# Value projections without a staging transpose, an early context sum, and a reordered output loop in an 8-core attention and gating kernel

## The chip, the cores and the metric

The kernel runs on all 8 cores of one Trainium2 chip. Each core computes one of the eight batch entries of 4096 tokens by 1024 features, with no exchange between cores. The metric is the device time in microseconds of the slowest core.

## The reference

Per batch entry (x is 4096 by 1024; 16 heads of 64; every token attends to every token, with an ALiBi bias that grows with the key's position):

```python
xn = _layernorm(x)
kqv = xn @ W_kqv.T                       # k, q, v
score = q @ k.T / sqrt(1024) + slope[h] * (n - s)
s = softmax(score) @ v
gf = global_net(xn.mean(tokens))         # 1024 -> 512 -> 256 -> 1
out = xn
for _ in range(3):
    tf = coupling_net(out)               # 1024 -> 1024 -> 512 -> 256 -> 1
    coupling = 0.1 + ar * (0.7 * gf + 0.3 * tf - 0.5) * 2.0
    out = out + coupling * twist(out)
x = x + s * silu(out)
```

## The kernel before

All stages use hand-placed buffers and hand-written semaphores. Each engine has one instruction stream, and each stream keeps the order in which the Python code emits it.

**Normalisation.** Tokens are loaded in slabs of 512, normalised, transposed by TensorE in 128x128 blocks, and cast by VectorE (L312) into XB, the bf16 transposed activations (features on partitions, 4096 tokens along the row).

**Attention.** Heads are worked in 8 pairs. `kqv_units(p, b)` is a generator that makes the projections of pair p, one unit for each `yield`. A "kq" unit is 8 accumulating matmuls of 512 tokens (L399) and one VectorE cast (L406). A "vt" unit is 8 accumulating matmuls (L416) that give V transposed for 512 tokens, a VectorE copy to VSTG (L423) and, emitted one unit later by `flush_vt`, four f32 transposes (L372) and two casts (L377) into the V buffer. `attn_units(p, b)` is the attention of pair p: for each block of 128 keys and each head two score matmuls (L474) and two exponentials on ScalarE (L482), and, one step later, two value matmuls a head (L456, L458). After each pass over the keys VectorE copies the sums out (L502). The four half banks of PA and PC form one ring (`ring_next`), which scores, projections and V transposes share. A unit or a score tile can start only when its half bank has been read.

Heads with steep slopes look at the last key blocks only. The first key block of a pair, N0_PAIR, is 30, 29, 27, 23, 15, 0, 0, 0 for pairs 0 to 7, of 32 blocks. So the pairs have 1, 1, 2, 3, 5, 8, 8, 8 vt units, 36 in all. The driving loop emits pair 0's units first, all at once, and then the units of pair p+1 between the steps of pair p, at 48/na units a step with na = 4 (34 - N0_PAIR[p]); a loop behind the steps emits what is left. V units come last in each pair's list.

**Context sum.** `gctx_chunk(p)` puts two VectorE sums over XB's rows (L321, 4096 elements each) behind each of the pairs 0 to 3; the eighth is followed by a small scaling. The result is used only after the attention.

**Feed-forward.** STATE, the f32 transposed activations, is rebuilt from x, and three cycles of 8 chunks of 512 tokens go through the coupling net (L721, L754, L775) and update STATE (L828, L837).

**Output.** 16 chunks of 256 tokens. ACT's queue loads the attention sums (SINB, 1024 KB, two buffers, L870). For each of 8 feature tiles: POOL multiplies STATE by SINB into FTMP (L881, two buffers), TensorE spreads the reciprocal of the softmax sums over the partitions (L893), VectorE multiplies the two into SG (L903, one buffer). Then for each half k of 128 tokens: SP loads the rows of x (XT, 512 KB, L914) as soon as the addition that last used this buffer is over, TensorE makes 8 transposes of SG (L921), VectorE adds (L929), SP stores (L933).

Of the kernel before, what the change touches and what calls it, by code (L numbers as in the profile page):

```python
# [6 lines left out]
F32 = mybir.dt.float32  # L7
BF16 = mybir.dt.bfloat16
AF = mybir.ActivationFunctionType
AOP = mybir.AluOpType  # L10

S, D, H, HD = 4096, 1024, 16, 64
NT = S // 128
NF = D // 128
# [3 lines left out]
NTC = S // TC  # L18
# [27 lines left out]
def build_program(debug=False):  # L46
# [76 lines left out]
    def at(name, shape, dtype, off_kib):  # L123
        t = nc.alloc_sbuf_tensor_at(name, shape, dtype, offset=A0 + int(off_kib * KIB))
        return t.ap()
# [7 lines left out]
    VB = [at(f"VB{i}", [128, 32 * 130], BF16, 144 + 8.25 * i) for i in range(2)]  # L133
    PB_ = [at(f"PBUF{i}", [128, 512], BF16, 160.5 + 1 * i) for i in range(12)]
    SRW = [at(f"SRW{i}", [128, 1024], F32, 172.5 + 4 * i) for i in range(2)]
    VSTG = [at(f"VSTG{i}", [128, 512], F32, 180.5 + 2 * i) for i in range(2)]
    vsj = [0]
    STATE = at("STATE", [128, NF * S], F32, 0)
    XT2s = [at(f"XT2s{i}", [128, 2 * D], F32, 128 + 8 * i) for i in range(2)]
    XNF2 = [at(f"XNF2{i}", [128, D], F32, 144 + 4 * i) for i in range(4)]  # L140
# [9 lines left out]
    TCF = 256  # L150
# [70 lines left out]
    with nc.Block() as block:  # L221
# [38 lines left out]
        for sl in range(NSLAB):  # L260
# [37 lines left out]
            for b in range(4):  # L298
                i = 4 * sl + b
                for g in range(2):  # L300
# [11 lines left out]
                    inst = VE.tensor_copy(out=dst, in_=src)  # L312
                    vXBe.inc(inst)
                    lnslot_tok[slot] = vXBe.n
        def gctx_chunk(pi):
            if pi >= 4:
                return
            if pi == 0:
                VE.wait_ge(vXBe.h, vXBe.n)
            for ft in range(2 * pi, 2 * pi + 2):  # L320
                VE.reduce_sum(gct[:, ft:ft + 1], XB[:, ft * S:(ft + 1) * S], axis=mybir.AxisListType.X)  # L321
            if pi == 3:
                VE.drain()
                inst = VE.tensor_scalar(out=gctb[:], in0=gct[:], scalar1=1.0 / S,
                                        scalar2=None, op0=AOP.mult)
                vGctx.inc(inst)

        TE.wait_ge(sW.h, W0_TOTAL)
        TE.wait_ge(sWG.h, WG_TOTAL)
# [9 lines left out]
        def ring_next():  # L339
            r = ring_pos[0]  # L340
            ring_pos[0] = (r + 1) % 4
            if ring_tok[r] is not None:
                sem, val = ring_tok[r]
                TE.wait_ge(sem.h, val)
            return r
# [8 lines left out]
        def kqv_units(p, b, prologue=False, prev2=None):  # L354
            first = [True]

            def gate_ve():
                if first[0]:
                    if prev2 is not None:
                        VE.wait_ge(tAV.h, pair_tok[prev2])  # L360
                    first[0] = False

            n0p = N0_PAIR[p]
            pvt = []

            def flush_vt():
                while pvt:
                    j, cp_tok, sc = pvt.pop(0)
                    r2 = ring_next()
                    TE.wait_ge(vKV.h, cp_tok)  # L370
                    for k in range(4):
                        inst = TE.transpose(RING[r2][:, k * 128:(k + 1) * 128],  # L372
                                            VSTG[j][:, k * 128:(k + 1) * 128], identf[:])
                    tKQ.inc(inst)
                    VE.wait_ge(tKQ.h, tKQ.n)
                    for hh in range(2):
                        inst = VE.tensor_copy(  # L377
                            out=v4[b][:, 4 * sc:4 * sc + 4, hh, 0:64],
                            in_=RING[r2].rearrange("p (k d) -> p k d", d=128)[:, :, hh * 64:hh * 64 + 64])
                        vKV.inc(inst)  # L380
                    ring_tok[r2] = (vKV, vKV.n)

            units = []
            for fpi, fp in enumerate([8 + p, p]):
                tc0 = (n0p * 128) // 512 if fpi == 1 else 0
                for tc in range(tc0, NTC):
                    units.append(("kq", fpi, fp, tc, 4 * (tc + 1)))
            for sc in range(n0p // 4, NTC):
                units.append(("vt", 0, 0, sc, 4 * (sc + 1)))
            if prologue:  # L390
                units.sort(key=lambda u: (u[4], u[0]))
            for kind, fpi, fp, tc, need in units:
                r = ring_next()
                if prologue:
                    TE.wait_ge(vXBe.h, min(2 * need, 64))
                if kind == "kq":
                    dst = QT[b] if fpi == 0 else KT[b]
                    for ft in range(NF):
                        inst = TE.matmul(RING[r],  # L399
                                         WK[:, ft * 3 * D + fp * 128: ft * 3 * D + (fp + 1) * 128],  # L400
                                         XB[:, ft * S + tc * 512: ft * S + (tc + 1) * 512],
                                         start=(ft == 0), stop=(ft == NF - 1))
                    tKQ.inc(inst)
                    gate_ve()
                    VE.wait_ge(tKQ.h, tKQ.n)
                    inst = VE.tensor_copy(out=dst[:, tc * 512:(tc + 1) * 512], in_=RING[r])  # L406
                    vKV.inc(inst)
                    ring_tok[r] = (vKV, vKV.n)
                    flush_vt()
                else:  # L410
                    sc = tc
                    base = 2 * D + p * 128
                    j = vsj[0] % 2
                    vsj[0] += 1
                    for ft in range(NF):
                        inst = TE.matmul(RING[r],  # L416
                                         WK[:, ft * 3 * D + base: ft * 3 * D + base + 128],
                                         XB[:, ft * S + sc * 512: ft * S + (sc + 1) * 512],
                                         start=(ft == 0), stop=(ft == NF - 1))
                    tKQ.inc(inst)  # L420
                    gate_ve()
                    VE.wait_ge(tKQ.h, tKQ.n)
                    inst = VE.tensor_copy(out=VSTG[j][:], in_=RING[r])  # L423
                    vKV.inc(inst)
                    ring_tok[r] = (vKV, vKV.n)
                    flush_vt()
                    pvt.append((j, vKV.n, sc))
                yield
            flush_vt()

        SC2 = 512
        NSCP = 4
# [87 lines left out]
        for p in range(8):  # L520
# [19 lines left out]
                    gen_k = None  # L540
            if p < 7:
                kqv_tok[p + 1] = vKV.n
            gctx_chunk(p)

        GP.wait_ge(tAV.h, tAV.n)
        GP.wait_ge(vSR.h, vSR.n)
# [317 lines left out]
        for tch in range(NTCF):  # L864
# [3 lines left out]
            if tch == 0:  # L868
# [3 lines left out]
                         .rearrange("(ft p) s -> p ft s", p=128)  # L872
                         ).then_inc(sSIND[sb6].h, 16)
            sSIND[sb6].n += 16
            for ft in range(NF):
                b2_ = sg_idx % 2
                GP.wait_ge(sSIND[sb6].h, sSIND[sb6].n)
# [13 lines left out]
                if sg_idx >= 4:  # L891
                    TE.wait_ge(vTT2.h, sg_idx - 4 + 1)
                inst = TE.matmul(HALF[slot][:, 0:TCF], sel[:, ft * 128:(ft + 1) * 128],  # L893
                                 RD[0:16, tch * TCF:(tch + 1) * TCF], start=True, stop=True)
                tRDB.inc(inst)
                VE.wait_ge(gTT1.h, gTT1.n)
                VE.wait_ge(tRDB.h, tRDB.n)
                if sg_idx == 0:
                    VE.wait_ge(vGF.h, RD_READY)
                if tch > 0 and ft == 0:  # L900
                    VE.wait_ge(tTRS.h, 2 * tch)
                SG = SG2[0]
                inst = VE.tensor_tensor(out=SG[:, ft * TCF:(ft + 1) * TCF],  # L903
                                        in0=FTMP[b2_][:], in1=HALF[slot][:, 0:TCF], op=AOP.mult)
                vTT2.inc(inst)
                sg_idx += 1
            for k in range(TCF // 128):
                tt = tch * (TCF // 128) + k
                b3_ = tt % 2
                if xt3_tok[b3_]:  # L910
                    SY.wait_ge(vOUT.h, xt3_tok[b3_])
                if tt == 0:
                    SY.wait_ge(vUPD.h, vUPD.n)
                SY.dma_start(out=XT3[b3_][:], in_=x_h[tt * 128:(tt + 1) * 128, :]  # L914
                             ).then_inc(sXT[b3_].h, 16); sXT[b3_].n += 16
                pt = [PC, PD][tt % 2]
                TE.wait_ge(vTT2.h, vTT2.n)
                if tt >= 2:
                    TE.wait_ge(vOUT.h, tt - 2 + 1)
                for ft in range(NF):  # L920
                    inst = TE.transpose(pt[:, ft * 128:(ft + 1) * 128],  # L921
                                        SG2[0][:, ft * TCF + k * 128: ft * TCF + (k + 1) * 128],
                                        identf[:])
                tTRS.inc(inst)
                VE.wait_ge(tTRS.h, tTRS.n)
                VE.wait_ge(sXT[b3_].h, sXT[b3_].n)
                if out_tok[b3_]:
                    VE.wait_ge(sOUTD[b3_].h, out_tok[b3_])
                inst = VE.tensor_tensor(out=OUT[b3_][:], in0=XT3[b3_][:], in1=pt[:], op=AOP.add)  # L929
                vOUT.inc(inst)  # L930
                xt3_tok[b3_] = vOUT.n
                SY.wait_ge(vOUT.h, vOUT.n)
                SY.dma_start(out=out_h[tt * 128:(tt + 1) * 128, :], in_=OUT[b3_][:]  # L933
                             ).then_inc(sOUTD[b3_].h, 16)
                sOUTD[b3_].n += 16
                out_tok[b3_] = sOUTD[b3_].n
        SY.wait_ge(sOUTD[0].h, sOUTD[0].n)
        SY.wait_ge(sOUTD[1].h, sOUTD[1].n)

# [57 lines left out]
```

## Time and profile before

| | us |
|---|---|
| median of 3 runs | 2844.83 |
| lowest, highest | 2834.77, 2899.36 |
| the profiled execution's own time | 2846.97 |
| its span (slowest core, core 7) | 2845.4 |
| spans of the eight cores | 2818.2 to 2845.4 |

The granted TensorE clock is a share of 2.4 GHz: 1.00 is 2.4 GHz and 0.50 is 1.2 GHz. In a timeline a row gives the start, the duration, the engine, the line, the operation, the tiles written and read, the shape and how many were merged; in brackets stands how long the engine sat idle before it, and what ended that. A matmul's duration is its latency; the spacing of the starts tells what it costs in a stream.

### The profile page before, as it was taken

To read this page: it belongs to the slowest core of one execution; us is meant where nothing else is said; L and a number is where in the kernel's file an instruction comes from. 1 tells how busy PE (TensorE), PEld (TensorE's weight loads), DVE (VectorE), ACT (ScalarE), POOL (GpSimd) and SP (SyncE) were. 2 spreads that over 40 slices of the span, in tenths; PEclk is the share of its full clock that TensorE was granted. 3 is DMA by queue.
4 is the path that set the end of the run, shared out by engine and by line. 5 is a ranking of instruction groups with operands and counts; after the bars stand their busy time and mean duration, and the time that the engine had idled before them with its cause. 6 is when DMAs were issued, how large, how long until landed. Compare 5 with 4: busy or idle time off the path is not lost.

```text
span 2845.4 us, 32583 instructions; the slowest of 8 cores (2818.2 to 2845.4 us)
## 1 busy us (share of the span) xinstructions
PE 2185.3 (77%) x8756; PEld 906.9 (32%) x8756; DVE 824.4 (29%) x1315; ACT 1465.9 (52%) x2366; POOL 100.7 (4%) x150
## 2 busy tenths in 40 slices
PE   0237879899899988999888855688888888854565
PEld 0233323232233223332222214433333333323444
DVE  1554432221111001100000006435435445345333
ACT  0222456668778888889999960133333333333000
POOL 1000000000000000000000000000000000002332
PEclk9669989899999899999999985799999999985555
DMA  9601110000000000000000024444454454434665
GB/s 182 167 30 31 31 31 16 16 8 16 8 8 8 8 8 9 1 8 9 8 9 8 8 56 145 129 109 110 93 117 106 93 114 104 100 78 128 192 194 176
DMA packets 343974, 190.21 MB, mean 67 GB/s; under 512 B 303419, under 2 KB 321981, under 8 KB 343694
## 3 DMA queue, kind: packets, MB, share of 16 engines
q1 hardware_dynamic: 323470, 160.08, 21.5%
q0 software_dynamic: 3696, 11.27, 2.9%
q10 hardware_dynamic: 16640, 16.78, 2.1%
q8 instruction: 85, 1.39, 0.2%
q14 instruction: 83, 0.68, 0.1%
HBM read 165.30 MB, written 36.96 MB: 71 GB/s over the span
## 4 chain that ended last, share of the span: by engine, by line
PE 46%; DVE 15%; ACT 15%; issue 11%; DMA 6%; DVEq 4%; POOL 1%; ACTq 1%; SPq 0%; another core or an unknown queue 0%; POOLq 0%
ACT PBUF L482 13%; PE PA L721 13%; PE PA L474 4%; PE PC L474 4%; PE PC L399 3%; PE PD L456 3%; PE PA L399 3%; DMA XT<-x 3%; PE PBp L456 3%; PE PD L458 3%; DVE STATE L837 2%; DVE TMP L828 2%; DVE SBF L806 2%; DVEq L840 2%; DVEq L834 2%
## 5 line engine op out<-in xcount | busy, mean ns | idle before, releaser
L482 ACT ACTIVATE PBUF<-PC,ebias_s 128x512 bf16<-128x512 f32 x973 | 670.9, 793 | 174.9 <-PE PC L474 117.6
L482 ACT ACTIVATE PBUF<-PA,ebias_s 128x512 bf16<-128x512 f32 x971 | 668.9, 789 | 157.7 <-PE PA L474 80.8
L474 PE MATMUL PC<-QT,KT 64*128 64x512 bf16 x973 | 351.6, 390 | 78.4 <-ACT PBUF L482 53.5
L721 PE MATMUL PA<-SBF,W1S 128*128 128x512 bf16 x1536 | 356.4, 395 | 25.5 <-DVE SBF L806 21.8
L474 PE MATMUL PA<-QT,KT 64*128 64x512 bf16 x971 | 325.0, 391 | 52.5 <-ACT PBUF L482 23.6
L732 ACT ACTIVATE H<-PA,b1c_s 128x512 bf16<-128x512 f32 x192 | 131.9, 687 | 344.9 <-PE PA L721 344.9
L502 DVE COPY SRW<-PBp 65x1024 f32<-65x1024 f32 x32 | 39.1, 1221 | 727.9 <-PE PD L458 727.9
L456 PE MATMUL PD<-PBUF,VB 128*65 128x512 bf16 x528 | 209.0, 396 | 29.2 <-ACT PBUF L482 15.6
L828 DVE TENSOR_TENSOR TMP<-PD,STATE 128x512 f32<-128x512 f32 x192 | 123.7, 686 | 359.7 <-PE PD L820 354.4
L721 PEld LDWEIGHTS PA<-SBF,W1S 128*128 128x128 bf16 x1536 | 153.7, 101 | 228.4 <-issue 65.2
L458 PE MATMUL PD<-PBUF,VB 128*65 128x512 bf16 x528 | 208.0, 394 | 0.0
L754 PE MATMUL PBp<-H,W2S 128*128 128x512 bf16 x768 | 174.9, 378 | 35.7 <-DMA W2S<-w2b_s 30.9
L474 PEld LDWEIGHTS PC<-QT,KT 64*128 64x128 bf16 x973 | 81.1, 94 | 320.5 <-issue 317.3
L456 PE MATMUL PBp<-PBUF,VB 128*65 128x512 bf16 x444 | 182.6, 411 | 0.2
L458 PE MATMUL PBp<-PBUF,VB 128*65 128x512 bf16 x444 | 172.0, 387 | 0.0
L474 PEld LDWEIGHTS PA<-QT,KT 64*128 64x128 bf16 x971 | 68.0, 94 | 275.2 <-issue 272.1
L765 ACT ACTIVATE H<-PBp,b2c_s 128x512 bf16<-128x512 f32 x96 | 66.0, 687 | 168.7 <-PE PBp L754 168.7
L306 PE MATMUL PA<-identf_s,XNF 128*128 128x128 f32 x128 | 27.4, 386 | 162.8 <-ACT XNF L293 162.8
L893 PE MATMUL PA<-RD,sel_s 16*128 16x256 f32 x128 | 58.3, 599 | 109.4 <-DVE SG L903 65.1
L837 DVE TENSOR_TENSOR STATE<-STATE,TMP 128x512 f32<-128x512 f32 x192 | 124.2, 688 | 7.6
L754 PEld LDWEIGHTS PBp<-H,W2S 128*128 128x128 bf16 x768 | 70.5, 97 | 147.8 <-issue 73.6
L399 PE MATMUL PC<-XB,WK 128*128 128x512 bf16 x400 | 98.2, 393 | 7.5 <-DVE QT L406 6.7
(109 smaller groups left out, 1846.1 us busy)
## 6 DMA issues: line engine op xcount, KB each, us to landing
W1S<-w1b_s SPq DMA_DIRECT2D x192, 256.0 KB, 2.9
W2S<-w2b_s SPq DMA_DIRECT2D x96, 256.0 KB, 2.8
XTs<-x SPq DMA_DIRECT2D x8, 2048.0 KB, 27.9
sraw_s<-SRW SPq DMA_DIRECT2D x64, 256.0 KB
XT2s<-x SPq DMA_DIRECT2D x16, 1024.0 KB, 5.9
XT<-x SPq DMA_DIRECT2D x32, 512.0 KB, 4.0
SINB<-sraw_s ACTq DMA_DIRECT2D x16, 1024.0 KB, 6.5
out<-OUT SPq DMA_DIRECT2D x32, 512.0 KB, 2.9
```

The lines of the kernel that those rows point to most:

```text
L399: inst = TE.matmul(RING[r], WK[:, ft * 3 * D + fp * 128: ft * 3 * D + (fp + 1) * 128], XB[:, ft * S + tc * 512: ft * S + (tc + 1) * 512], ...
L456: TE.matmul(OUTH[hh][0], v4[b][:, pnt, hh, 0:65], PB_[s0][:], start=st, stop=stop)
L458: inst = TE.matmul(OUTH[hh][1], v4[b][:, pnt, hh, 0:65], PB_[s0 + 1][:], start=st, stop=stop)
L474: inst = TE.matmul(RING[r], lhs, QT[b][hh * 64:(hh + 1) * 64, sc * SC2:(sc + 1) * SC2], start=True, stop=True)
L482: inst = SE.activation(out=PB_[slot][:], in_=RING[r], func=AF.Exp, bias=ebias[:, h * 32 + nt: h * 32 + nt + 1], scale=1.0 / 32.0)
L721: inst = TE.matmul(HALF[slot][:], W1S[wslot][:, ft * 128:(ft + 1) * 128], sbf[:, ft * TC:(ft + 1) * TC], start=(ft == 0), stop=(ft == NF - 1))
L732: inst = SE.activation(out=h1buf[:, f1 * TC:(f1 + 1) * TC], in_=HALF[slot][:], func=AF.Gelu, bias=b1c[:, f1:f1 + 1])
L754: inst = TE.matmul(HALF[slot][:], W2S[w2slot][:, f1t * 128:(f1t + 1) * 128], H1[:, f1t * TC:(f1t + 1) * TC], start=(f1t == 0), stop=(f1t = ...
L765: inst = SE.activation(out=H2[:, f2 * TC:(f2 + 1) * TC], in_=HALF[slot][:], func=AF.Gelu, bias=b2c[:, f2:f2 + 1])
L828: inst = VE.tensor_tensor(out=TMP[ii % 2][:], in0=PD[:, 512:1024], in1=STATE[:, jj * S + col: jj * S + col + TC], op=AOP.mult)
L837: inst = VE.tensor_tensor(out=STATE[:, ii * S + col: ii * S + col + TC], in0=STATE[:, ii * S + col: ii * S + col + TC], in1=TMP[ii % 2][:] ...
L893: inst = TE.matmul(HALF[slot][:, 0:TCF], sel[:, ft * 128:(ft + 1) * 128], RD[0:16, tch * TCF:(tch + 1) * TCF], start=True, stop=True)
```

## The change

There are three parts.

1. The context sum: the eight sums of L321 and the scaling are emitted right behind the normalisation, ahead of pair 0's projections. `gctx_chunk` is gone.
2. V: the vt unit is replaced by a "v" unit for each block of 128 tokens. It has 8 matmuls with XB's 128x128 block as the weights and 128 columns of WK moving, and one VectorE cast of 128x128 straight into the V buffer. VSTG, the copy to it, the f32 transposes and `flush_vt` are gone. The pairs have 2, 3, 5, 9, 17, 32, 32, 32 v units, 132 in all. The rate of 48/na stays.
3. The output loop: both loads of x stand at the head of a chunk; the two transposes of a feature tile are emitted behind the spreading matmul of the next tile; both additions and stores stand at the end.

```diff
-        def gctx_chunk(pi):
...
+        VE.wait_ge(vXBe.h, vXBe.n)
+        for ft in range(NF):
+            VE.reduce_sum(gct[:, ft:ft + 1], XB[:, ft * S:(ft + 1) * S], axis=mybir.AxisListType.X)
+        VE.drain()
+        inst = VE.tensor_scalar(out=gctb[:], in0=gct[:], scalar1=1.0 / S, scalar2=None, op0=AOP.mult)
+        vGctx.inc(inst)
...
-            for sc in range(n0p // 4, NTC):
-                units.append(("vt", 0, 0, sc, 4 * (sc + 1)))
+            for tt in range(n0p, NT):
+                units.append(("v", 0, 0, tt, tt + 1))
...
                     for ft in range(NF):
-                        inst = TE.matmul(RING[r],
+                        inst = TE.matmul(RING[r][:, 0:128],
+                                         XB[:, ft * S + tt * 128: ft * S + (tt + 1) * 128],
                                          WK[:, ft * 3 * D + base: ft * 3 * D + base + 128],
-                                         XB[:, ft * S + sc * 512: ft * S + (sc + 1) * 512],
                                          start=(ft == 0), stop=(ft == NF - 1))
                     tKQ.inc(inst)
                     gate_ve()
                     VE.wait_ge(tKQ.h, tKQ.n)
-                    inst = VE.tensor_copy(out=VSTG[j][:], in_=RING[r])
-                    vKV.inc(inst)
-                    ring_tok[r] = (vKV, vKV.n)
-                    flush_vt()
-                    pvt.append((j, vKV.n, sc))
+                    inst = VE.tensor_copy(out=v4[b][:, tt, :, 0:64],
+                                          in_=RING[r][:, 0:128].rearrange("p (h d) -> p h d", h=2))
+                vKV.inc(inst)
+                ring_tok[r] = (vKV, vKV.n)
                 yield
...
+            for k in range(2):
+                tt = 2 * tch + k
+                if xt3_tok[k]:
+                    SY.wait_ge(vOUT.h, xt3_tok[k])
+                if tt == 0:
+                    SY.wait_ge(vUPD.h, vUPD.n)
+                SY.dma_start(out=XT3[k][:], in_=x_h[tt * 128:(tt + 1) * 128, :]
+                             ).then_inc(sXT[k].h, 16); sXT[k].n += 16
+            pxp = []
+            def flush_xp(tch=tch):
+                while pxp:
+                    ft, tok = pxp.pop(0)
+                    TE.wait_ge(vTT2.h, tok)
+                    if ft == 0 and tch >= 1:
+                        TE.wait_ge(vOUT.h, 2 * tch)
+                    for k in range(2):
+                        inst = TE.transpose([PC, PD][k][:, ft * 128:(ft + 1) * 128],
+                                            SG2[0][:, ft * TCF + k * 128: ft * TCF + (k + 1) * 128],
+                                            identf[:])
+                    if ft == NF - 1:
+                        tTRS.inc(inst, 2)
...
                 tRDB.inc(inst)
+                flush_xp()
...
                 vTT2.inc(inst)
+                pxp.append((ft, vTT2.n))
...
+            flush_xp()
+            for k in range(2):
+                tt = 2 * tch + k
+                if k == 0:
+                    VE.wait_ge(tTRS.h, 2 * (tch + 1))
+                VE.wait_ge(sXT[k].h, sXT[k].n)
+                if out_tok[k]:
+                    VE.wait_ge(sOUTD[k].h, out_tok[k])
+                inst = VE.tensor_tensor(out=OUT[k][:], in0=XT3[k][:], in1=[PC, PD][k][:], op=AOP.add)
```

## Rows read from the trace of the kernel before

**Rows 1.** The page: its first line, and busy time of the engines.

```profile
span 2845.4 us, 32583 instructions; the slowest of 8 cores (2818.2 to 2845.4 us)
PE 2185.3 (77%) x8756; PEld 906.9 (32%) x8756; DVE 824.4 (29%) x1315; ACT 1465.9 (52%) x2366; POOL 100.7 (4%) x150
```

**Rows 2.** Windows, core 7: busy us by engine, granted clock, DMA share, GB/s.

```profile
630.00:1684.00 1054.00, 949.24 (x3688) 308.61 (x3686) 86.04 (x127) 932.55 (x1592) 0.00 (x0) 0.97 0.04 8
...
2586.00:2845.00 259.00, 162.34 (x512) 123.37 (x512) 90.18 (x160) 0.00 (x0) 88.95 (x126) 0.56 0.57 185
```

**Rows 3.** Waits of VectorE from 2586 us on: total us, times, longest.

```profile
DVE OUT L929 <- DMA XT<-x: 88.9, 16, 7.0
```

**Rows 4.** The line L929: durations in ns, first and last start.

```profile
L929 DVE TENSOR_TENSOR OUT<-XT,PC x16: 1220/1222/1222, 2596.0 to 2835.2; 128x1024 f32<-128x1024 f32 x16
L929 DVE TENSOR_TENSOR OUT<-XT,PD x16: 1220/1221/1222, 2602.9 to 2841.2; 128x1024 f32<-128x1024 f32 x16
```

**Rows 5.** Timeline of one chunk of the output loop, all engines.

```profile
2691.81 1.22 DVE L929 TENSOR_TENSOR OUT<-XT,PC 128x1024 f32<-128x1024 f32 x1 [2.44 <-PE PC L921]
...
2693.53 0.38 SPq L914 DMA_DIRECT2D XT<-x  x1
...
2699.94 1.22 DVE L929 TENSOR_TENSOR OUT<-XT,PD 128x1024 f32<-128x1024 f32 x1 [6.91 <-DMA XT<-x]
2701.08 0.74 DVE L903 TENSOR_TENSOR SG<-FTMP,PA 128x256 f32<-128x256 f32 x2
...
2706.14 0.42 DVE L903 TENSOR_TENSOR SG<-FTMP,PBp 128x256 f32<-128x256 f32 x1 [0.27 <-POOL FTMP L881]
...
2706.81 1.94 PE L921 MATMUL PC<-identf_s,SG 128*128 128x128 f32 x8 [1.42 <-DVE SG L903]
...
2708.55 1.69 PE L921 MATMUL PD<-identf_s,SG 128*128 128x128 f32 x8
2709.00 1.22 DVE L929 TENSOR_TENSOR OUT<-XT,PC 128x1024 f32<-128x1024 f32 x1 [2.44 <-PE PC L921]
```

**Rows 6.** Timeline of an earlier chunk: the spreading matmuls at clock 0.50.

```profile
2677.17 2.07 PE L893 MATMUL PA<-RD,sel_s 16*128 16x256 f32 x4
...
2679.04 1.91 PE L893 MATMUL PBp<-RD,sel_s 16*128 16x256 f32 x4
```

**Rows 7.** Windows of one chunk while its transfers run, columns as before.

```profile
2605.00:2608.00 3.00, 3.00 (x8) 2.07 (x7) 1.59 (x4) 0.00 (x0) 2.89 (x5) 0.50 0.99 339
2610.00:2618.00 8.00, 7.16 (x24) 5.55 (x23) 1.22 (x1) 0.00 (x0) 0.42 (x1) 0.50 0.85 258
```

**Rows 8.** Timelines around the context sums, of VectorE and of TensorE.

```profile
209.38 1.28 DVE L312 CAST XB<-PBp 128x512 bf16<-128x512 f32 x2
...
268.65 8.73 DVE L321 TENSOR_REDUCE gct<-XB 128x1 f32<-128x4096 bf16 x2
...
278.13 1.18 PE L474 MATMUL PA<-QT,KT 64*128 64x512 bf16 x2 [7.29 <-DVE QT L406]
...
337.08 3.57 PE L399 MATMUL PC<-XB,WK 128*128 128x512 bf16 x8 [6.75 <-DVE QT L406]
```

**Rows 9.** Timeline of TensorE: a step without and a step with a vt unit.

```profile
619.85 0.41 PE L456 MATMUL PBp<-PBUF,VB 128*65 128x512 bf16 x1
...
621.72 0.41 PE L456 MATMUL PBp<-PBUF,VB 128*65 128x512 bf16 x1
...
622.61 1.89 PE L416 MATMUL PC<-XB,WK 128*128 128x512 bf16 x8
624.34 0.60 PE L372 MATMUL PA<-identf_s,VSTG 128*128 128x128 f32 x4
...
626.60 0.41 PE L456 MATMUL PBp<-PBUF,VB 128*65 128x512 bf16 x1
```

**Rows 10.** Windows of L482 alone: ScalarE busy, clock, DMA (kq units, vt units).

```profile
730.00:830.00 100.00, 79.19 (x134) 1.00 0.03 6
830.00:905.00 75.00, 56.79 (x95) 1.00 0.04 8
```

More of the change, by code:

```diff
@@ L135, in build_program @@
     SRW = [at(f"SRW{i}", [128, 1024], F32, 172.5 + 4 * i) for i in range(2)]
-    VSTG = [at(f"VSTG{i}", [128, 512], F32, 180.5 + 2 * i) for i in range(2)]
-    vsj = [0]
     STATE = at("STATE", [128, NF * S], F32, 0)
@@ L314, in build_program @@
                     lnslot_tok[slot] = vXBe.n
-        def gctx_chunk(pi):
[L316 to L326, printed above, removed]
+        VE.wait_ge(vXBe.h, vXBe.n)
[4 more added lines that the diff above has]
+        vGctx.inc(inst)
         TE.wait_ge(sW.h, W0_TOTAL)
@@ L363, in kqv_units @@
             n0p = N0_PAIR[p]
[L364 to L379, printed above, removed]
-                        vKV.inc(inst)
-                    ring_tok[r2] = (vKV, vKV.n)
             units = []
@@ L406, in kqv_units @@
                     inst = VE.tensor_copy(out=dst[:, tc * 512:(tc + 1) * 512], in_=RING[r])
-                    vKV.inc(inst)
-                    ring_tok[r] = (vKV, vKV.n)
-                    flush_vt()
                 else:
-                    sc = tc
+                    tt = tc
                     base = 2 * D + p * 128
-                    j = vsj[0] % 2
-                    vsj[0] += 1
                     for ft in range(NF):
-                        inst = TE.matmul(RING[r],
+                        inst = TE.matmul(RING[r][:, 0:128],
+                                         XB[:, ft * S + tt * 128: ft * S + (tt + 1) * 128],
                                          WK[:, ft * 3 * D + base: ft * 3 * D + base + 128],
-                                         XB[:, ft * S + sc * 512: ft * S + (sc + 1) * 512],
                                          start=(ft == 0), stop=(ft == NF - 1))
@@ L422, in kqv_units @@
                     VE.wait_ge(tKQ.h, tKQ.n)
-                    inst = VE.tensor_copy(out=VSTG[j][:], in_=RING[r])
-                    vKV.inc(inst)
-                    ring_tok[r] = (vKV, vKV.n)
-                    flush_vt()
-                    pvt.append((j, vKV.n, sc))
+                    inst = VE.tensor_copy(out=v4[b][:, tt, :, 0:64],
+                                          in_=RING[r][:, 0:128].rearrange("p (h d) -> p h d", h=2))
+                vKV.inc(inst)
+                ring_tok[r] = (vKV, vKV.n)
                 yield
-            flush_vt()
         SC2 = 512
@@ L542, in build_program @@
                 kqv_tok[p + 1] = vKV.n
-            gctx_chunk(p)
         GP.wait_ge(tAV.h, tAV.n)
@@ L901, in build_program @@
                     VE.wait_ge(tTRS.h, 2 * tch)
-                SG = SG2[0]
-                inst = VE.tensor_tensor(out=SG[:, ft * TCF:(ft + 1) * TCF],
+                inst = VE.tensor_tensor(out=SG2[0][:, ft * TCF:(ft + 1) * TCF],
                                         in0=FTMP[b2_][:], in1=HALF[slot][:, 0:TCF], op=AOP.mult)
                 vTT2.inc(inst)
+                pxp.append((ft, vTT2.n))
                 sg_idx += 1
[L907 to L929, printed above, removed]
@@ L930, in build_program @@
+            flush_xp()
[7 more added lines that the diff above has]
+                inst = VE.tensor_tensor(out=OUT[k][:], in0=XT3[k][:], in1=[PC, PD][k][:], op=AOP.add)
                 vOUT.inc(inst)
-                xt3_tok[b3_] = vOUT.n
+                xt3_tok[k] = vOUT.n
@@ L932, in build_program @@
                 SY.wait_ge(vOUT.h, vOUT.n)
[L933 to L936, printed above, removed]
+                SY.dma_start(out=out_h[tt * 128:(tt + 1) * 128, :], in_=OUT[k][:]
+                             ).then_inc(sOUTD[k].h, 16)
+                sOUTD[k].n += 16
+                out_tok[k] = sOUTD[k].n
         SY.wait_ge(sOUTD[0].h, sOUTD[0].n)
```

## The prediction

> **What bounds the kernel now.** I read the page first. TensorE is busy for 77% of the span and ScalarE for 52% [rows 1]: an average over stages that are bound by different things, so I took windows by stage. The change touches two of them. From pair 4 on, attention keeps ScalarE busy for 932.55 of 1054 us and TensorE for 949.24 [rows 2]; the exponentials set the pace, and ScalarE is idle where projection units hold TensorE up. In the output loop (259 us) no engine is busy for more than 63%, and the DMA engines are at a share of 0.57 [rows 2]: a loop of waits.
>
> The reader should see that loop in the waits, then in one chunk. VectorE sat idle for 88.9 us until a load of x had landed, 16 times [rows 3]. From one addition on PD to that of the next chunk it takes (2841.2 - 2602.9) / 15 = 15.9 us [rows 4]. In the chunk shown the addition on PC starts at 2691.81; the load of the other half is issued only at 2693.53, though nothing in it depends on the chunk's work; the addition on PD starts at 2699.94, and the next chunk's eight multiplications stand behind it, from 2701.08 to 2706.56, then come 16 transposes in a block, and only then the next addition, at 2709.00 [rows 5].
>
> **Part 1, the context sum.** Eight sums of 4.37 us (8.73 for two) [rows 8], 35 us of VectorE in either kernel. Before, each couple stands in front of casts that the shared ring waits for: TensorE sat idle for 7.29 and 6.75 us behind the first two couples [rows 8], and for 6.9 and 5.8 behind the other two, 26.8 us in all. After each, the clock is down and a unit takes 3.57 us where a warm one takes 1.89 [rows 8, 9], some 1.7 us more, 7 in all. So the old place costs about 34 us.
>
> In the new place the sums start when the last cast to XB is over, at 209.38 + 1.28 = 210.7, and end at 245.7; the first unit's cast ends at 246.4. TensorE fills the four ring places until 216.1 and then has nothing: 30.3 us idle, and one slow restart of 1.7 us, 32 us. The part is worth 34 - 32 = **2 us**. Queued behind the sums are pair 0's casts, and behind these its scores and all of ScalarE's work; nothing covers them. Bounds: with no slow restart on either side 26.8 - 30.3, a loss of 3.5; with all restarts 2.5 us long, a gain of 4.
>
> **Part 2, V.** A step with a vt unit takes 4.88 us (621.72 to 626.60), one without takes 1.87 us (619.85 to 621.72) [rows 9]; so a vt unit costs TensorE's stream 3.0 us: 8 matmuls for 1.73, four transposes for 0.53 (624.34 to 624.87), the rest waits for VectorE to clear a ring place. Where the exponentials set the pace, part of that is hidden: in the vt window ScalarE sat idle for 75 - 56.79 = 18.2 us at 8 units and a bit of another, **2.2 us a unit**; in the kq window 20.8 us at 15 units, 1.4 a unit [rows 10]. A kq unit costs 1.73 and about 0.4 of waiting. So about 0.75 us of any unit is free.
>
> No row shows a bf16 matmul with 128 moving columns and new weights each time. From below: a quarter of the 512-column spacing of 0.217 us, 0.054, so 0.43 us for a unit of 8. From above: the f32 128x128 transposes load as many weights of twice the size and move as many columns, 0.15 us each (0.60 for four) [rows 9], so 1.2. I find no reason that it is near either end and take the middle, **0.8 us**, and 0.25 for its wait for a small cast, 1.05 in all.
>
> The Trainium skill ("TensorE: Matmul & The Clock Gate", section on the back-to-back issue gap) gives about 81 ns a matmul sustained at 128 columns; no row here shows it. By that a unit would be 0.65 us, and the sum for this part, by the steps below, 45 us instead of 24.
>
> Units for pairs 5, 6 and 7, made under pairs 4 to 6: before, 24 vt at 2.2 us = 53 us of idle ScalarE. After, 96 v units at 1.05 - 0.75 = 0.3: 29 us. The rate of 48/na now leaves 3, 2 and 2 of the 48 units behind the last step of these pairs, with nothing beside them: 7 x 1.05 = 7 us. Net 17. Units for pairs 0 to 4, where TensorE's own stream sets the pace: 12 vt at 3.0 = 36, 36 v at 0.8 = 29, net 7. The part gives **24 us**. At 0.43 a unit: 53 - 5 late, 36 - 15 early, 69. At 1.2: 53 - 67 - 10 late, 36 - 43 early, a loss of 31. VectorE's work falls (one cast of a quarter's size for each v unit against a copy and two casts), and it was busy for 86 of 1054 us [rows 2], so that is worth nothing.
>
> **Part 3, the output loop.** What bounds a chunk once the loads are early? First TensorE, at clock 0.50: 8 spreading matmuls at 0.47 (four in 1.87) [rows 6] and 16 transposes at 0.22 (eight in 1.74) [rows 5], 7.2 us. The first two spreading matmuls (0.9) run beneath the additions, so 6.3 us are on the path. In front stand the first multiplication and its release, 0.42 + 0.25 (2706.14 + 0.42 to 2706.81); between tiles, four times about 0.15 where a transpose waits for its multiplication, 0.6; behind the last transpose 0.45 until the addition (the eighth starts at 2706.81 + 7 x 0.22 = 2708.33, the addition at 2709.00, less its own 0.22); then two additions at 1.14 (2699.94 to 2701.08) [rows 5], 2.3. Sum **10.3 to 10.5 us**. POOL's eight products at 0.73 lie inside. The transposes, which were 3.5 us of their own, cost only what they put between the spreading matmuls. SP's stores wait in the same queue as the loads, so the next loads are issued about 0.5 and 0.9 us after the second addition and have 8 us to land; the one shown, issued at 2693.53, was awaited until 2699.94, 6.4 us.
>
> Second, the transfers: 1024 KB of sums, two loads and two stores of 512 KB, 3.15 MB a chunk. At 339 GB/s, share 0.99, that is 9.3 us; at 258 GB/s, the long stretch with a share of 0.85, 12.2 us [rows 7]. The two bounds lie close to each other, and I take **11.2 us**, between 10.5 and 12.2. From chunk to chunk that saves 15.9 - 11.2 = 4.7, 15 times, 70. In the first chunk the load can run under the reciprocal, for another 7. Together **77 us**. At 9.6 a chunk it would be 101, at 13, 50.
>
> The clock could help: in this loop it is 0.56 on average [rows 2], and if it rose, the spreading matmuls would take 0.24 each and TensorE would be no bound, but the 9.3 us of the transfers remain. The same page of the Trainium skill (Part 4, on transposes) says that transposes don't count as activity for the clock; the low clock in a loop busy for 63% agrees. By that the 10.5 stands, without it the sum gains at most 15 x 1.2 = 18 us.
>
> **The sum.** 2 + 24 + 77 = 103. From the profiled execution's own 2846.97 us (span 2845.4 and 1.6 around it) to **2744 us**. That execution is 2 us above the median of the three runs, so against the median I say 2742.
>
> **Rivals.** (a) *The transfers stretch.* All eight cores ask for more at once, and the loads land late at any pace; chunks of 12.5 to 14.5. For it: the stretch at 258 GB/s. Against it: 339 GB/s with all cores in the same stage. At 13.5 the loop gives 43 us: 2847 - 2 - 24 - 43 = 2778. (b) *The output loop doesn't shrink*: the rate of 185 GB/s is all that the cores together get, and the wait only moves from the load of x to another transfer. Against it speak the single stretches at twice the others' rate. 2847 - 26 = 2821. (c) *V is dear*, the case of the other sign. If a matmul with fresh weights costs 0.216 us, as the transposes do at the low clock [rows 5], a v unit is 1.7 us. Late: 53 - 96 x 1.2 - 14 = -76; early: 36 - 61 = -25; a loss of 101 against gains of 79, so 2869. It decides from about 1.5 us a unit on, and needs the clock to fall while v units run; the step shown has it at full speed. [...] (d) *Both better*: v units near 0.5 us and chunks of 9.6: 2847 - 2 - 66 - 101 = 2678.
>
> **How the numbers follow.** Forecast (chunks of 10.3 to 12.4, v units of 0.6 to 1.1) 0.63, its own range 2710 to 2775. Rival (a) 0.15, (b) 0.06, (c) 0.08 in all its degrees (0.02 of it above the time before by over 2%), (d) 0.08. The range of 2700 to 2790 leaves out (b), (c) and the better half of (d), about 2 in 10. Faster by over 2% means below 2788 (2% is about what a measurement of this kernel can tell from no change): the forecast, (a), (d), and a little of (c), 0.87. Within 2%: 0.11. Slower: 0.02.
>
> **What would show it.** In the waits, the idle time of L929 for loads of x falls from 88.9 to under 20 us, and additions on PD follow each other at 10.5 to 12 us. If the DMA share in that loop reads 0.8 or more, the transfers are the bound. TensorE sits idle for one piece of about 30 us near 216 us and never again for 6 to 7 us behind a sum. v matmuls start 0.08 to 0.12 us apart, and ScalarE's idle time per 25 us in the v stretch falls from 6 us to about 2. I am wrong if the spacing is above 0.15, if chunks stay above 13 us, or if the early sums cost more than the 34 us that they free.

## The result: less than half of what was forecast, and the profile after

| | before | after |
|---|---|---|
| ratio of after to before | 1 | 0.9827, 95% interval 0.9787 to 0.9866 |
| profiled execution, us | 2846.97 | 2791.05 |
| its span, us | 2845.4 | 2789.5 |
| medians of 10 executions, us | 2847.62 | 2819.76 |

The change makes the kernel 1.7% faster, some 49 us (38 to 61). I had forecast 103 us. The median after is further up than the profiled execution because some executions of either kernel run with one die at a lower clock; the ratio compares executions without that.

By stage, from the two traces: attention ends at 1643 instead of 1682 us, 39 us earlier, and the output loop takes 247 instead of 259 us, 12 us less. I had forecast 26 for the first (2 + 24) and 77 for the second. So the error that made the forecast too large sits in part 3.

The output loop after: the line of the final additions (ns, first and last start), the waits of VectorE from 2542 us on, and a window of 100 us (columns as in [rows 2]) beside the same window of the kernel before. The first fence is of after:

```profile
L904 DVE TENSOR_TENSOR OUT<-XT,PD x16: 1211/1214/1216, 2557.9 to 2785.2; 128x1024 f32<-128x1024 f32 x16
...
DVE SG L891 <- PE PBp L881: 93.5, 64, 1.8
DVE SG L891 <- PE PA L881: 44.9, 34, 1.5
DVE OUT L904 <- PE PD L857: 16.7, 16, 1.1
...
2600.00:2700.00 100.00, 91.36 (x212) 42.30 (x210) 37.38 (x67) 0.00 (x0) 37.55 (x53) 0.50 0.68 216
```

And of before:

```profile
2600.00:2700.00 100.00, 61.06 (x192) 46.31 (x192) 33.85 (x61) 0.00 (x0) 33.86 (x48) 0.55 0.61 194
```

No addition waits for a load of x any more, where it was 88.9 us [rows 3]; that step was right. But additions on PD now stand (2785.2 - 2557.9) / 15 = 15.15 us apart, against 15.9 [rows 4]. In place of the load VectorE waits for the spreading matmuls (138 us). TensorE is busy for 91 us of 100 instead of 61, and the transfers are at a share of 0.68.

One tile of that loop, TensorE alone (start, duration, line, tiles):

```profile
2652.96 1.22 PE L881 MATMUL PBp<-RD,sel_s 16*128 16x256 f32 x2
...
2654.10 0.47 PE L857 MATMUL PC<-identf_s,SG 128*128 128x128 f32 x1
...
2654.37 0.42 PE L857 MATMUL PD<-identf_s,SG 128*128 128x128 f32 x1
...
2654.72 1.22 PE L881 MATMUL PA<-RD,sel_s 16*128 16x256 f32 x2
```

The reader should see "x2": one spreading matmul of the source is two instructions. None of these rows has idle time in brackets, so TensorE waits for no other engine between them. A tile takes 2654.72 - 2652.96 = 1.76 us, of which 1.14 goes to the spreading matmul (until the first transpose starts) and 0.62 to two transposes.

Attention after: TensorE at the new place of the sums, then a v unit and what follows it.

```profile
211.01 3.62 PE L372 MATMUL PC<-XB,WK 128*128 128x512 bf16 x16
244.83 6.37 PE L372 MATMUL PA<-XB,WK 128*128 128x512 bf16 x16 [30.20 <-DVE QT L379]
...
817.33 0.61 PE L384 MATMUL PA<-WK,XB 128*128 128x128 bf16 x8
817.87 0.60 PE L440 MATMUL PC<-QT,KT 64*128 64x512 bf16 x2
```

TensorE is idle for 30.20 us in front of pair 0, as worked out (30.3). A v unit holds it for 0.54 us (817.33 to 817.87), 0.068 for a matmul.

### The profile page after: what moved, and what is told of

Same layout as the page of the kernel before. It is cut to its first block, busy times and chain, and to the rows that moved or that the text cites. A ratio compares the mean times of both kernels' runs of the same rounds, so it can differ in the third digit from the quotient of the medians.

```text
span 2789.5 us, 34004 instructions; the slowest of 8 cores (2771.9 to 2789.5 us)
## 1 busy us (share of the span) xinstructions
PE 2213.6 (79%) x9380; PEld 908.9 (33%) x9380; DVE 810.1 (29%) x1339; ACT 1468.2 (53%) x2366; POOL 102.2 (4%) x150
## 4 chain that ended last, share of the span: by engine, by line
PE 54%; ACT 14%; DVE 14%; issue 10%; DVEq 5%; DMA 3%; ACTq 1%; SPq 0%; another core or an unknown queue 0%; POOL 0%; POOLq 0%
PE PA L686 13%; ACT PBUF L448 12%; PE PC L440 5%; PE PA L440 5%; PE PA L372 3%; PE PD L422 3%; PE PC L372 3%; PE PBp L422 3%; PE PD L424 3%; PE PBp L881 3%; DVE STATE L802 2%; DVE TMP L793 2%; DVE SBF L771 2%; PE PA L881 2%; DVEq L805 2%
## 5 line engine op out<-in xcount | busy, mean ns | idle before, releaser
L448 ACT ACTIVATE PBUF<-PC,ebias_s 128x512 bf16<-128x512 f32 x979 | 656.3, 752 | 177.5 <-PE PC L440 124.3
L448 ACT ACTIVATE PBUF<-PA,ebias_s 128x512 bf16<-128x512 f32 x965 | 646.9, 750 | 115.2 <-PE PA L440 57.2
L440 PE MATMUL PC<-QT,KT 64*128 64x512 bf16 x979 | 345.3, 386 | 65.4 <-ACT PBUF L448 46.3
L372 PE MATMUL PA<-XB,WK 128*128 128x512 bf16 x424 | 106.1, 398 | 30.2 <-DVE QT L379 30.2
L881 PE MATMUL PA<-RD,sel_s 16*128 16x256 f32 x128 | 72.0, 689 | 46.7 <-DVE RD L820 46.7
```

Of the source, the lines that this page charges most:

```text
L372: inst = TE.matmul(RING[r], WK[:, ft * 3 * D + fp * 128: ft * 3 * D + (fp + 1) * 128], XB[:, ft * S + tc * 512: ft * S + (tc + 1) * 512], ...
L440: inst = TE.matmul(RING[r], lhs, QT[b][hh * 64:(hh + 1) * 64, sc * SC2:(sc + 1) * SC2], start=True, stop=True)
L448: inst = SE.activation(out=PB_[slot][:], in_=RING[r], func=AF.Exp, bias=ebias[:, h * 32 + nt: h * 32 + nt + 1], scale=1.0 / 32.0)
```

## The experiments

All ratios are against the kernel before on the same chip, with 95% intervals; 1% is 28.5 us. First the three parts, each alone.

**Part 1 alone.**

```diff
-        def gctx_chunk(pi):
...
+        for ft in range(NF):
+            VE.reduce_sum(gct[:, ft:ft + 1], XB[:, ft * S:(ft + 1) * S], axis=mybir.AxisListType.X)
```

> Part 1 of the change alone, on the kernel before. Theory (the recorded step): the early sums cost 32 us at the start of attention and free 34 us behind pairs 0 to 3, so 2 us faster, within 4 us either way; pair 0 then ends about 30 us later than before, pair 3 about 0 us later. Rival: the four old stalls were partly free, because the exponentials had work queued; then this part alone is 5 to 15 us slower.

Ratio 1.001 (0.999 to 1.0031): nothing, as recorded. On core 1 the first copy of each pair's last pass starts at 298.5, 350.0, 419.8 and 530.0 us for pairs 0 to 3, against 266.6, 325.2, 404.8 and 524.6 before: 32 us late at pair 0, then 25, 15 and 5, and 1 at pair 4. The four old places that are now empty give back 7, 10, 10 and 4 us, 31 in all. The rival that the old stalls were partly free falls.

**Part 2 alone.**

```diff
-            for sc in range(n0p // 4, NTC):
-                units.append(("vt", 0, 0, sc, 4 * (sc + 1)))
+            for tt in range(n0p, NT):
+                units.append(("v", 0, 0, tt, tt + 1))
```

(with the unit's body and without VSTG and `flush_vt`, as in the change.)

> Part 2 alone. The recorded step says 24 us faster (v unit 0.8 us of TensorE). Theory after the trace of the changed kernel: a v unit takes 0.54 us there (eight matmuls from 817.33 to 817.87), so 30 to 45 us faster. Rival: most of what pairs 1 to 3 gained there came from the sums being gone, and this part gives 20 us or less.

Ratio 0.9878 (0.9857 to 0.99), 35 us (28 to 41). By the same marks on core 1, and from the first projection matmul for pair 0: pair 0 with its units takes 52.2 us against 57.5, pairs 1 to 3 take 54.5, 73.6, 112.7 against 58.6, 79.6, 119.8. That is 22 us in the pairs where TensorE sets the pace. Pairs 4 to 6 take 183.7, 308.3, 337.4 against 194.4, 313.0, 346.1, 24 us less, and pair 7, in which nothing was changed, 308.9 against 303.1, 6 more. As a mean of the eight cores it is 22 less in pairs 4 to 6 and 4.5 more in pair 7.

**Part 3 alone.**

```diff
                 tRDB.inc(inst)
+                flush_xp()
```

(with the loads at the head and the additions at the end, as in the change.)

> Part 3 alone. The recorded step says 77 us faster. Theory after the trace: 12 to 17 us faster, because the chunk takes 15.15 us instead of 15.9: each spreading matmul is two instructions of 0.47 us at the low clock, so 0.93 us and not 0.47, and alternating them with transposes adds 0.4 us a tile. Rival: part 3 gives much more alone and loses it next to the other two parts.

Ratio 0.9983 (0.9963 to 1.0003): about 5 us (-1 to 11), not clear of noise and less than the 12 to 17 expected. The additions on PD, and the window of the same stretch:

```profile
L939 DVE TENSOR_TENSOR OUT<-XT,PD x16: 1212/1214/1216, 2591.0 to 2818.3; 128x1024 f32<-128x1024 f32 x16
...
2600.00:2700.00 100.00, 91.36 (x211) 42.65 (x212) 37.52 (x67) 0.00 (x0) 37.84 (x53) 0.50 0.69 208
```

Chunks are 15.15 us, as beside the other parts. The three parts add to -0.1 + 1.2 + 0.2 = 1.3% against 1.7% (1.3 to 2.1) of the whole; each has an interval of 0.2 either way, so no effect of one part on another shows beyond the noise.

**The transposes back in a block.** One thing of part 3 undone.

```diff
                 tRDB.inc(inst)
-                flush_xp()
...
-                    ft, tok = pxp.pop(0)
-                    TE.wait_ge(vTT2.h, tok)
...
+                    for k in range(2):
+                        for ft in range(NF):
+                            inst = TE.transpose([PC, PD][k][:, ft * 128:(ft + 1) * 128],
...
+                        tTRS.inc(inst)
...
-                if k == 0:
-                    VE.wait_ge(tTRS.h, 2 * (tch + 1))
+                VE.wait_ge(tTRS.h, 2 * tch + k + 1)
```

> Part 3 with one thing undone: the loads of x stay at the head of the chunk and the additions at its end, but the 16 transposes stand again in one block behind the eighth multiplication, eight for the first half and then eight for the second. If TensorE and the alternation set the pace of the output loop: TensorE needs 8 x 0.93 + 16 x 0.22 = 11 us a chunk plus about 1 us of waiting for the last multiplication, so chunks of 12 us and 55 to 65 us faster than before. If the transfers set the pace (rival a on record), nothing is gained over part 3 as it is: chunks stay at 15 us, 12 to 17 us faster than before.

Ratio 0.9763 (0.9749 to 0.9776), 67 us faster. The line of the additions, what they wait for, and the window:

```profile
L937 DVE TENSOR_TENSOR OUT<-XT,PD x16: 1220/1222/1222, 2594.0 to 2763.2; 128x1024 f32<-128x1024 f32 x16
...
  DMA XT<-x: 18.9, 10
...
2600.00:2700.00 100.00, 85.06 (x291) 64.27 (x289) 50.88 (x90) 0.00 (x0) 51.00 (x72) 0.60 0.97 277
```

Chunks are (2763.2 - 2594.0) / 15 = 11.28 us, and the DMA engines are at 0.97. Rival (a), that the transfers stretch the chunks to 12.5 us or more, falls. The early loads were worth 62 us more than part 3 showed; the alternation of transposes and spreading matmuls took them back.

The window has one more difference, a granted clock of 0.60 on average where part 3 had 0.50. Behind a block of transposes the clock is up for a few us:

```profile
2659.77 0.93 PE L893 MATMUL PD<-identf_s,SG 128*128 128x128 f32 x4
2660.63 1.13 PE L916 MATMUL PA<-RD,sel_s 16*128 16x256 f32 x4
```

These four instructions take 0.96 us, until the next group starts at 2661.59; at 0.50 four take 1.87 [rows 6]. So e4 alone doesn't tell how much of the gain is the clock's; the next run does.

**Two groups of transposes.**

```diff
                 tRDB.inc(inst)
-                flush_xp()
+                if ft == 4:
+                    flush_xp()
```

> Part 3 with the transposes in two groups of eight (four tiles each), behind the fifth spreading matmul and behind the last multiplication, instead of in eight groups of two. If the 0.4 us a tile comes from alternating between transposes and spreading matmuls, four changes of kind a chunk instead of sixteen leave it near e4: chunks of 12 us, 50 to 65 us faster than before. If it comes from spreading matmuls that can't run ahead past a transpose which waits for VectorE, the two groups keep a part of it: chunks of 13 to 14 us, 30 to 45 us faster.

Ratio 0.9783 (0.9766 to 0.98), 62 us faster. The line of the additions and the window (core 0):

```profile
L940 DVE TENSOR_TENSOR OUT<-XT,PD x16: 1214/1220/1222, 2593.6 to 2767.1; 128x1024 f32<-128x1024 f32 x16
...
2600.00:2700.00 100.00, 98.66 (x278) 69.52 (x277) 49.09 (x87) 0.00 (x0) 48.78 (x69) 0.50 0.89 263
```

Chunks are 11.57 us, at a clock of 0.50 throughout, with the same instructions as in part 3. So most of the price was the eight-fold change of kind and not the clock; spreading matmuls that can't run past a waiting transpose cost little. TensorE is busy for 98.66 of 100 us here: its 11.0 us of work a chunk (8 x 0.93 + 16 x 0.22) nearly fill the chunk.

**A lighter spreading matmul, alternation kept.**

```diff
+        inst = VE.tensor_copy(out=RDt[:], in_=RD[:])
+        inst = VE.tensor_copy(out=RDb[:], in_=RDt[:])
+        inst = VE.tensor_copy(out=selb[:], in_=sel[:])
...
-                inst = TE.matmul(HALF[slot][:, 0:TCF], sel[:, ft * 128:(ft + 1) * 128],
-                                 RD[0:16, tch * TCF:(tch + 1) * TCF], start=True, stop=True)
+                inst = TE.matmul(HALF[slot][:, 0:TCF], selb[:, ft * 128:(ft + 1) * 128],
+                                 RDb[0:16, tch * TCF:(tch + 1) * TCF], start=True, stop=True)
```

> Part 3 as in the change, with the reciprocals and the selection matrix of the spreading matmul in bf16 (three small casts ahead of the loop, the result is rounded more coarsely); the alternation with the transposes stays. If TensorE's stream sets the pace, a tile drops from 1.77 us by about 0.7 (one instruction of 0.21 instead of two of 0.47 at the low clock) to about 1.05, and a chunk from 15.15 to 10 or 11.3 us, where the transfers bind: 50 to 65 us faster than before. If the transfers or the round between the engines set the pace at 15 us, it stays at 5 to 10 us faster.

Ratio 0.9772 (0.9752 to 0.9792), 65 us faster. The reciprocals are rounded more coarsely than in the other kernels. TensorE:

```profile
2644.23 0.42 PE L905 MATMUL PD<-identf_s,SG 128*128 128x128 f32 x1
2644.58 0.39 PE L929 MATMUL PBp<-RDb,selb 16*128 16x256 bf16 x1
2644.90 0.47 PE L905 MATMUL PC<-identf_s,SG 128*128 128x128 f32 x1
...
2645.52 0.39 PE L929 MATMUL PBp<-RDb,selb 16*128 16x256 bf16 x1
...
L952 DVE TENSOR_TENSOR OUT<-XT,PD x16: 1212/1220/1222, 2593.6 to 2765.7; 128x1024 f32<-128x1024 f32 x16
```

"x1": the bf16 matmul is one instruction, the tile takes 0.94 us instead of 1.76, and the chunks fall to (2765.7 - 2593.6) / 15 = 11.5 us. So TensorE's stream set the pace of part 3.

**What binds at 11.5 us.** e6 with a part of its traffic left out: from the second chunk on half of each load of x is missing, so that this part of the output is not the reference's.

```diff
-                SY.dma_start(out=XT3[k][:], in_=x_h[tt * 128:(tt + 1) * 128, :]
+                cw = D if tch == 0 else D // 2
+                SY.dma_start(out=XT3[k][:, 0:cw], in_=x_h[tt * 128:(tt + 1) * 128, 0:cw]
```

> e6 with half of each load of x left out from the second chunk on (512 of 1024 columns; the other half of the buffer keeps the first chunk's rows, so that part of the output is not the reference's). A chunk moves 2.62 MB instead of 3.15. If the transfers bind e6 at 11.5 us (its additions waited 28 us for loads of x), a chunk falls to 9.6 to 10 us, 22 to 28 us faster than e6, 88 to 94 us faster than before. If what binds e6 is the round of TensorE and VectorE, chunks stay at 11.3 or more, at most 5 us faster than e6.

Ratio 0.9714 (0.9686 to 0.9743), 81 us (73 to 89) faster than before, some 16 more than e6 with its 65 (59 to 70). The additions on PD of e9:

```profile
L953 DVE TENSOR_TENSOR OUT<-XT,PD x16: 1211/1214/1216, 2596.1 to 2750.4; 128x1024 f32<-128x1024 f32 x16
...
2600.00:2700.00 100.00, 72.82 (x234) 29.10 (x233) 53.93 (x97) 0.00 (x0) 55.62 (x78) 0.50 0.78 252
```

and what they waited for in e6:

```profile
  DMA XT<-x: 28.0, 12
  PE PD L905: 6.3, 5
```

Chunks fall from 11.5 to 10.3 us, 18 us over the loop, and no addition waits for a load any more; behind the loads the round of the engines comes next. The gain is less than the 22 to 28 us expected, and the chunk 0.3 us longer than the upper of the two lengths expected: the engines' own round was nearer than I had put it.

**The sums where nobody waits.**

```diff
-            if pi >= 4:
+            if pi != 6:
                 return
-            for ft in range(2 * pi, 2 * pi + 2):
+            for ft in range(NF):
```

> The kernel before with the eight context sums moved behind pair 6 instead of behind pairs 0 to 3. Pair 7 has no projection units of another pair beside it, and VectorE's next work there is the copy at the end of the first pass, some 75 us later, so the 35 us of sums should block nobody. Theory: the old place cost 34 us, so 30 to 36 us faster than before. Rival: the old stalls were hidden in part, since moving the sums to the front in one piece changed nothing although it leaves TensorE idle for 30 us; then 10 to 20 us.

Ratio 0.9893 (0.9876 to 0.9911), 30 us (25 to 35) faster. VectorE's timeline (start, duration; in brackets the idle time before it):

```profile
1345.45 34.69 DVE L320 TENSOR_REDUCE gct<-XB 128x1 f32<-128x4096 bf16 x8
1380.22 0.17 DVE L323 TENSOR_SCALAR gctb<-gct 128x8 bf16<-128x8 f32 x1
1418.52 1.22 DVE L501 COPY SRW<-PBp 65x1024 f32<-65x1024 f32 x1 [38.13 <-PE PD L457]
```

All eight sums lie in a stretch in which VectorE had nothing else to do, and still has 38 us to spare. This agrees with the 34 us that I gave the old place.

**All three together: part 2, the block of e4, the sums of e5.**

> Part 2 of the change, the output loop of e4 and the sums behind pair 6 together. If the three gains add (35 + 67 + 30 to 36), 130 to 138 us faster than before, about 2705 us, ratio 0.953. If the parts share a cause, for instance if the sums' old stalls cost less once the V units are short, 110 to 120 us.

Ratio 0.9513 (0.9492 to 0.9534), 138 us (132 to 144) faster, a median of 2700 us. The gains add within the noise: 1.22 + 2.37 + 1.07 = 4.66% alone, 4.87% together. It beats both kernels, and does the same arithmetic as the change. Once more, in another set of runs:

> e8 once more, beside the next run on the same chip: 0.951 of the kernel before, within its interval of 0.002.

Ratio 0.9502 (0.9471 to 0.9533). With e6's bf16 spreading on top:

> e8 with the bf16 spreading of e6. If e8's output loop is bound by transfers (share 0.94), TensorE's lighter work is worth nothing: the same as e8 within 5 us, some 135 to 145 us faster than before. If TensorE still binds part of it, 10 to 15 us faster than e8.

Ratio 0.9546 (0.9518 to 0.9574), 129 us (121 to 137) faster than before: no gain over e8, if anything a loss. The chunks of e8 are (2689.0 - 2517.3) / 15 = 11.45 us at a DMA share of 0.94, and e10's additions wait for loads of x as e8's do:

```profile
L908 DVE TENSOR_TENSOR OUT<-XT,PD x16: 1220/1222/1222, 2517.3 to 2689.0; 128x1024 f32<-128x1024 f32 x16
...
  DMA XT<-x: 31.3, 16
```

So with the transposes in a block the transfers set the pace, and a lighter TensorE is worth nothing.

**The units left behind a pair's last step.**

```diff
-            nk = 48
+            nk = 51
```

> e8 with the rate of projection units raised from 48/na to 51/na a step, so that none of pairs 5, 6 and 7's 48 units is left behind the last step of the pair before. The trace of e2 has pair 7 5.8 us longer than before although nothing in it was changed, and two units stand in front of it. If the left units cost that much at each of three places, 8 to 17 us faster than e8. If they cost what was recorded (7 us in all), 5 to 7 us. If pair 7's extra time comes from a low clock and not from the units, nothing.

Ratio 0.949 (0.9451 to 0.9528) against e11's 0.9502 (0.9471 to 0.9533): 3 us, inside the noise. In the profiles, on core 1, pair 7 takes 303.0 us against 306.0 in e11, and pair 6 335.7 against 337.5. Over the eight cores the means are 303.3 against 307.0 and 334.5 against 337.3, and pair 7 is shorter on each core. So the units left behind pair 6 cost pair 7 some 4 us, which is its whole loss in e2 (303.0 before, 307.5 in e2). Pairs 1 to 3 get some 3 us longer at the higher rate, and the attention as a whole ends 4 us earlier; the times can't show that little.

## Why the prediction was wrong, step by step

**Part 1, right.** Forecast 2 us (-3.5 to 4), measured -3 (-9 to 3). The idle piece of 30.3 us came out at 30.20, and its slow restart is there, 2.75 us and not 1.7 (6.37 us for two units that take 3.62 warm). e5 and e1 show that the old places cost about what the stalls and slow restarts add to, 30 (25 to 35) and 31 us against 34.

**Part 2, right in sign, too small, and the terms wrong both ways.** Forecast 24 us, measured 35 (28 to 41). That it came out this near is partly luck: one term was too dear, another too cheap. The v unit was put at 0.8 us, the middle of 0.43 and 1.2; it takes 0.54, near the bound from below. Where TensorE sets the pace, 12 x 3.0 - 36 x 0.54 = 17 us would follow, and 22 were measured on core 1, instead of 7. Under pairs 4 to 6 the 2.2 us of a vt unit less almost nothing for a v unit should have given more than 40 us, and 24 less 6 were there (22 less 4.5 as a mean of the cores).

A part of the gap is the price of 2.2 us, which was read from a window with the end of a pass in it. Two windows of before show that price (ScalarE busy, clock), and the second of them a loss that is there without any unit:

```profile
839.00:879.00 40.00, 31.85 (x54) 1.00 0.00 1
...
955.00:980.00 25.00, 17.60 (x30) 0.64 0.10 22
```

Both are of core 7. In the first, inside a pass, ScalarE sat idle for 8.15 us, with a vt unit every 9.08 us: 1.85 a unit, 44 us for 24 units instead of 53. Two windows of after, both with v units, show where those still cost:

```profile
820.00:845.00 25.00, 24.68 (x44) 1.00 0.00 1
845.00:870.00 25.00, 16.40 (x28) 0.69 0.10 22
```

Inside a pass the idle time is 0.3 us in 25, against the 2 us that I expected. The second window holds the end of a pass (the copies out start at 852.6). There a score matmul waits for a v cast that stands behind those copies on VectorE, the clock falls, and TensorE runs at 0.50 for some 20 us. But the kernel before has the same drop at the end of a pass, from about 962 us on, when no unit is left: 7.4 us idle in its window against 8.6 in this one. So the v cast is at most a small part of that loss. It costs in other places, as at the two units left behind pair 6:

```profile
1335.47 1.05 PE L384 MATMUL PC<-WK,XB 128*128 128x128 bf16 x16
1338.91 0.67 PE L440 MATMUL PA<-QT,KT 64*128 64x512 bf16 x2 [2.39 <-DVE VB L391]
```

e12's traces put these left units at some 4 us in pair 7 and 3 in pair 6, where 7 in all were forecast. What makes the rest of the gap stays open.

The Trainium skill's 81 ns for a matmul of 128 columns ("TensorE: Matmul & The Clock Gate", back-to-back issue gap) would have given 45 us; the trace has 68 ns at full clock, so the page errs to the dear side here, and the sum by it was too high because of the 2.2 us a vt unit and what stays open above.

**Part 3, wrong.** Forecast 77 us, measured 5 (-1 to 11) alone and 12 in the traces of the whole change. The step that failed is "8 spreading matmuls at 0.47 (four in 1.87)". The rows of [rows 6] say x4 and I took four matmuls of the source; they are two, with two instructions each. The profile had it: the view of line L893 counts 128 records on PA and 128 on PBp, 256 for 16 x 8 = 128 matmuls, and the window in [rows 2] has 512 records of TensorE for these and 256 transposes. So TensorE needed 8 x 0.93 + 16 x 0.22 = 11.0 us a chunk before any waiting, and in a chunk of before it was already busy for that long, at a clock of 0.50:

```profile
2603.00:2619.00 16.00, 11.10 (x32) 8.24 (x32) 5.57 (x10) 0.00 (x0) 5.63 (x8) 0.50 0.62 197
```

The second error in that step is that alternating was free but for 0.6 us. A tile of 0.93 + 0.43 = 1.36 us takes 1.76. Put into the recorded sum of 10.3 us, the first error adds 2.8 us (six matmuls on the path at 0.46 more) and the second about 2; that is most of the way to 15.15. The chunk of after then adds up: 0.67 to the first transpose, six tiles of 1.76, 0.74 for the last, 0.91 until the addition, 2.27 for the two additions, 15.15 us, as measured. With e6's tile of 0.94 the same sum gives 10.2 us, and e9 measured 10.3. Either error alone would have cost little: e4 and e7 keep the dear matmul without most of the alternation, e6 the alternation without the dear matmul, and all three come down to 11.3 to 11.6 us. The price of the transfers was near: 11.2 us forecast, a choice between 10.5 and 12.2, and 11.28 in e4, 11.5 in e6 and 11.45 in e8 at DMA shares of 0.90 to 0.97. The 7 us of the first chunk were not had either: from the first spreading matmul to the first addition on PD it takes 15.3 us after against 16.8 before, and 11.7 in e4.

Of the rivals none named this. (b), a loop that doesn't shrink, comes near the outcome by the wrong cause: the wait moved from the load to TensorE and not to another transfer.

## What to carry to other kernels

Before a stage's engine time is summed, count the records of a line against the calls in the source, and hold the sum against that engine's busy time in one period: here both said 11 us for a loop that I took to need 7. A price for one unit that is read from a window must come from a window that holds nothing else. Moving a load off the path shows its worth only if nothing is put on the path with it; interleaving short operations of two kinds on TensorE cost 0.4 us each round and ate 62 us, and a block of the same instructions kept them. A long VectorE operation without a hurry belongs behind the last work that others wait for: the same 35 us cost 30 to 34 in one place, as much in another and nothing that shows in a third.

## What the runs showed of the hardware

An f32 matmul of 16 x 128 weights and 256 columns is two instructions of 0.47 us at 1.2 GHz, 0.93 us for both; the bf16 one is a single instruction, and a round of it and two transposes takes 0.94 us (e6). A change from transposes to f32 matmuls of this kind and back costs 0.4 us at 1.2 GHz (1.76 us a round against 1.36); why was not tested.

In the two-group loop TensorE was busy for 98.66 of 100 us, with f32 transposes and f32 spreading matmuls, and the granted clock stayed at 0.50 (1.2 GHz). The Trainium skill ("TensorE: Matmul & The Clock Gate", Part 4) says that transposes don't count as activity for the clock. The low clock of this loop fits that, although half of its records are matmuls, but other rows speak against it as a rule, and the prediction's "agrees" was said too soon. In e4's output loop the clock came up behind a block of 16 transposes. And in the normalisation of the kernel before (core 1), where TensorE had been idle for 12.23 us and then made nothing but f32 transposes from 203.71 us on, the distance of their starts falls from 0.21 to 0.11 us and the granted clock rises from 0.50 to 1.00:

```profile
205.45 1.92 PE L306 MATMUL PBp<-identf_s,XNF 128*128 128x128 f32 x8
207.16 1.28 PE L306 MATMUL PA<-identf_s,XNF 128*128 128x128 f32 x8
208.27 1.04 PE L306 MATMUL PBp<-identf_s,XNF 128*128 128x128 f32 x8
```

At DMA shares of 0.93 to 0.98 the eight cores moved 266 to 277 GB/s each in e4, all at once (2600 to 2700 us). The Trainium skill ("HBM Reference", Specifications) gives about 358 GB/s a core with both cores of a pair active; sums in rows of 1 KB, x and the output in rows of 4 KB, loads, stores and two queues mixed reached 77% of that at most.
